# A fused Mamba block and 16-expert layer on one core: the late expert weights in small waited pieces, and a last group normalised on VectorE

## What is computed

```
attn:  xz = layernorm(x) @ in_proj.T;  x_in, z = split(xz)
       u = silu(causal_conv4(x_in) + conv_b);  delta, B, C = u @ x_proj.T
       h_t = h_{t-1} * exp(-delta_t) + B_t u_t;  y_t = h_t . C_t
       out = (y * silu(z)) @ out_proj.T + x
ffn:   the two best of 16 experts for each token, weights w from their softmax
       for each expert e:  y = (silu(x @ W1[e]) * (x @ W3[e])) @ W2[e]
                           out += w_e * (layernorm(y) * gamma[e] + beta[e])
```

## Time and profile before

| | us |
|---|---|
| median of 3 runs (971.96 to 977.71) | 974.45 |
| the profiled execution, its own time | 974.93 |
| its span, first to last instruction | 973.1 |
| TensorE busy | 940.0 (97%) |
| VectorE busy | 722.8 (74%) |
| ScalarE busy | 689.5 (71%) |
| GpSimd busy | 620.4 (64%) |

### The profile page before, as it was taken

How to read it: one execution, slowest core, us unless ns; L and a number is a source line. 1 busy time by engine, 2 the same in 40 slices (tenths; PEclk the granted TensorE clock), 3 DMA queues, 4 the chain that set the end, 5 groups by cost and what they waited for, 6 DMA issues and landing times.

```text
span 973.1 us, 26657 instructions
## 1 busy us (share of the span) xinstructions
PE 940.0 (97%) x7207; PEld 833.9 (86%) x7207; DVE 722.8 (74%) x2524; ACT 689.5 (71%) x1358; POOL 620.4 (64%) x813
## 2 busy tenths in 40 slices
PE   8999999999999999998879999999999999999994
PEld 5777887788887887887879999999999999999951
DVE  2379999999999998898623767776767677677656
ACT  3777787777778778765115777777777778778536
POOL 2445777777778777775541666666666666566647
PEclk9999999999999999999988999999999999999997
DMA  4001323121111111110865211111111111111075
GB/s 136 12 12 34 93 93 97 58 62 48 55 56 53 53 43 42 42 42 22 324 238 175 87 44 51 49 51 46 49 50 48 47 50 49 42 53 50 18 293 225
DMA packets 54159, 75.25 MB, mean 77 GB/s; under 512 B 11103, under 2 KB 32865, under 8 KB 53376
## 3 DMA queue, kind: packets, MB, share of 16 engines
q1 hardware_dynamic: 42784, 54.87, 18.4%
q0 software_dynamic: 8672, 16.93, 4.8%
q10 hardware_dynamic: 2560, 1.75, 0.6%
HBM read 47.09 MB, written 27.41 MB: 77 GB/s over the span
## 4 chain that ended last, share of the span: by engine, by line
PE 79%; DVE 7%; POOL 6%; issue 5%; DMA 1%; ACT 1%; POOLq 0%; DVEq 0%; SPq 0%; ACTq 0%
PE pA L1886 11%; PE pR L1886 11%; PE pA L1472 11%; PE pB L1894 6%; PE pY L1894 5%; PE pY L1586 4%; PE pB L1498 3%; PE pB L1632 3%; PE pA L1487 3%; PE pY L1622 3%; PE pA L1443 3%; POOL chosen_scratch L656 2%; PE pY L1605 2%; PE pY L1554 2%; PE pR L1570 2%
## 5 line engine op out<-in xcount | busy, mean ns | idle before, releaser
L656 POOL DMA_INDIRECT chosen_scratch<-yo,got_id x143 | 146.8, 1027 | 93.7 <-issue 87.9
L961 ACT ACTIVATE stage<-w_sb 128x1024 f32 x143 | 151.2, 1057 | 55.7 <-issue 55.6
L1358 DVE TENSOR_TENSOR hidT<-pR,sil 128x512 f32<-128x512 f32 x143 | 98.9, 692 | 81.0 <-ACT sil L956 60.8
L595 POOL DMA_INDIRECT slots_scratch<-xrow,send_at x128 | 134.7, 1052 | 35.3 <-issue 31.3
L1886 PE MATMUL pA<-xsT,stage 128*128 128x128 f32 x1144 | 151.3, 275 | 0.4 <-ACT xsT L945 0.4
L1886 PE MATMUL pR<-xsT,stage 128*128 128x128 f32 x1144 | 151.1, 275 | 0.0
L1886 PEld LDWEIGHTS pA<-xsT,stage 128*128 128x128 f32 x1144 | 139.2, 192 | 0.7 <-ACT xsT L945 0.6
L1886 PEld LDWEIGHTS pR<-xsT,stage 128*128 128x128 f32 x1144 | 139.0, 192 | 0.0
L1472 PE MATMUL pA<-xn,taps 128*128 128x512 f32 x256 | 129.8, 594 | 1.0 <-ACT xn L722 1.0
L646 POOL TENSOR_TENSOR ers<-eve,neg_half 128x1 f32<-128x1 f32 x143 | 81.7, 571 | 57.2 <-DVE eve L1370 40.0
L956 ACT ACTIVATE sil<-pA 128x512 f32<-128x512 f32 x143 | 85.3, 596 | 26.5 <-PE pA L1886 21.7
(11 more groups left out here) (198 smaller groups left out, 2102.0 us busy)
## 6 DMA issues: line engine op xcount, KB each, us to landing
got<-slots_scratch SPq DMA_DIRECT2D x143, 65.0 KB, 1.9
w_sb<-chosen_scratch SPq DMA_DIRECT2D x16, 512.0 KB, 5.4
w_sb<-in_w_dram SPq DMA_DIRECT2D x1, 6144.0 KB
xin<-in_x_dram SPq DMA_DIRECT2D x16, 256.0 KB
xr<-in_x_dram SPq DMA_DIRECT2D x16, 256.0 KB, 3.1
x_scratch<-x SPq DMA_DIRECT2D x16, 256.0 KB
w_sb<-in_w_dram SPq DMA_DIRECT2D x4, 1024.0 KB, 7.2
fx<-x_scratch SPq DMA_DIRECT2D x1, 4096.0 KB
```

What stands on the lines that cost most here:

```text
L595: eng.indirect_dma_start(slots_d, bass.IndirectOffsetOnAxis(ap=send_at[:, s % 2, k, t:t + 1], axis=0), xrow[:, s % 2, k, t, :], None).then ...
L656: eng.indirect_dma_start(chosen_d, bass.IndirectOffsetOnAxis(ap=got_id[:, j % NGOT:j % NGOT + 1], axis=0), yo[:, q, :], None, bounds_check ...
L961: eng.activation(stage[:, j % NSTAGE, :, :].rearrange("p k f -> p (k f)"), w13_sb[:, bass.ds(e, 1), :, :].rearrange("p o k f -> p (o k f)" ...
L1358: eng.tensor_tensor(hidT[:, p, :], pR[:, p, :], sil[:, p, :], ALU.mult).then_inc(hid_ready, 1)
```

## The change

- `load_late` is replaced. `load_middle(e0, e1)` issues the weights of two experts (1 MB) and first waits until the piece before has landed (`w13_loaded`). The first, (4, 6), waits also for the state products of the last sequence (`ys_mm`). Five such pieces take experts 4 to 13; then come `store_x1(15)`, expert 14 alone, and `load_last`: expert 15, gamma, and beta, the last one after a wait until gamma has landed.
- `tail_at` is computed in the last call of `positions`, right behind the counts and ahead of `placed` and `pos`, no longer behind `count_i`.
- `fnm` is gone. GpSimd multiplies the mean itself with `frs`, and the second operation subtracts the product from `shift3` where it added before.
- Group 15 is normalised by VectorE with four `tensor_scalar`s from PSUM, added by VectorE, and stored by a DMA of ScalarE's queue; GpSimd's addition, ScalarE's four activations and SyncE's store of it are gone.
- 42 fillers in place of 46.

```diff
-DVE_ADDS = tuple(range(1, 15, 2))
+DVE_ADDS = tuple(range(1, 16, 2))
...
+            def load_middle(e0, e1):
+
+                if e0 == 4:
+                    eng.wait_ge(ys_mm, 2 * NS)
+                eng.wait_ge(w13_loaded, 16 * (e0 // 2 - 1))
+                load_w13(e0, e1)
+
+            def load_last():
+                eng.wait_ge(y_step, 11 * NS)
+                eng.wait_ge(w13_loaded, 16 * 7)
+                load_w13(15, NE)
+                for k, v in enumerate((gamma, beta)):
+                    if k:
+                        eng.wait_ge(gb_loaded, 16 * k)
                     eng.dma_start(gb[:, k, :, :], ...).then_inc(gb_loaded, 16)
...
             store_x1(14)
-            load_late()
+            load_middle(4, 6)
+            load_middle(6, 8)
+            load_middle(8, 10)
+            load_middle(10, 12)
+            load_middle(12, 14)
             store_x1(15)
+            load_middle(14, 15)
+            load_last()
...
-                eng.tensor_tensor(fshift[:, h % 2, c], fnm[:, h % 2, c], frs[:, h % 2, c], ALU.mult).then_inc(f_rstd, 1)
+                eng.tensor_tensor(fshift[:, h % 2, c], fmv[:, h % 2, c, 0:1].rearrange("p t o -> p (t o)"), frs[:, h % 2, c], ALU.mult).then_inc(f_rstd, 1)
...
-                eng.tensor_tensor(fshift[:, h % 2, c], fshift[:, h % 2, c], shift3[:, g:g + n, :].rearrange("p g t -> p (g t)"), ALU.add).then_inc(f_rstd, 1)
+                eng.tensor_tensor(fshift[:, h % 2, c], shift3[:, g:g + n, :].rearrange("p g t -> p (g t)"), fshift[:, h % 2, c], ALU.subtract).then_inc(f_rstd, 1)
...
-            eng.wait_ge(w13_loaded, 32)
+            eng.wait_ge(w13_loaded, 16 * 8)
...
-            for h in range(len(PARTS)):
+            for h in range(len(PARTS) - 1):
                 last_norm(h)
+            eng.wait_ge(f_o_dve, len(DVE_ADDS) + 1)
+            eng.dma_start(ov[NG - 1, :, :, :], fx1[:, NG - 1, :, :]).then_inc(f_stored, 16)
...
+                if s == NS - 1:
+                    eng.wait_ge(rank_read, NS)
+                    eng.tensor_scalar(tail_at[:, :], running[:, :], slot_no[:, 0:1], None, ALU.add).then_inc(tail_ready, 1)
...
-                eng.tensor_scalar(fnm[:, h % 2, c], fmv[:, h % 2, c, 0:1].rearrange("p t o -> p (t o)"), -1.0, None, ALU.mult).then_inc(f_var, 1)
...
+            h = len(PARTS) - 1
+            g = NG - 1
+            eng.wait_ge(f_rstd, 3 * h + 3)
+            eng.wait_ge(f_o_dve, len(DVE_ADDS))
+            for t in range(NT4):
+                eng.tensor_scalar(fn[:, h % 2, 0, t, :], sum_bank(g)[:, tile(t)], frs[:, h % 2, t:t + 1], fshift[:, h % 2, t:t + 1], ALU.mult, ALU.add).then_inc(f_last, 1)
+            eng.wait_ge(f_last, NT4)
+            eng.tensor_tensor(fx1[:, g, :, :], fn[:, h % 2, 0, :, :], fx1[:, g, :, :], ALU.add).then_inc(f_o_dve, 1)
...
-            keep_warm(46)
+            keep_warm(42)
```

More of the change, by code:

```diff
@@ L256, in sandwich @@
         fve = sb("fve", [P, 2, 2 * NT4])
-        fnm = sb("fnm", [P, 2, 2 * NT4])
         frs = sb("frs", [P, 2, 2 * NT4])
@@ L316, in sandwich @@
         cv = chosen_d.rearrange("(k g p t) d -> g p k (t d)", p=P, t=NT4, k=2)
+        ov = out.rearrange("s (p t) d -> s p t d", t=NT4)
         sum_bank = lambda g: w13_sb[:, 0, 0, :] if g == 0 else (pA, pB, pR, pY)[g % 8 // 2][:, g % 2, :]
@@ L349, in sandwich @@
         f_sum, f_moments, f_var, f_rstd, f_n, f_o = sem("f_sum"), sem("f_moments"), sem("f_var"), sem("f_rstd"), sem("f_n"), sem("f_o")
-        f_o_dve = sem("f_o_dve")
+        f_o_dve, f_last = sem("f_o_dve"), sem("f_last")
         f_stored = sem("f_stored")
@@ L380, in load_late @@
                 for k, v in enumerate((gamma, beta)):
+                    eng.dma_start(gb[:, k, :, :], v.rearrange("(o e) d -> o e d", o=1).broadcast_to([P, NE, D])).then_inc(gb_loaded, 16)
+            def load_middle(e0, e1):
[10 more added lines that the diff above has]
+                        eng.wait_ge(gb_loaded, 16 * k)
                     eng.dma_start(gb[:, k, :, :], v.rearrange("(o e) d -> o e d", o=1).broadcast_to([P, NE, D])).then_inc(gb_loaded, 16)
@@ L483, in _ @@
                 eng.wait_ge(stored[q], len(range(q, NSLOT, 4)) * 16)
-            ov = out.rearrange("s (p t) d -> s p t d", t=NT4)
             eng.wait_ge(staged, NSLOT)
@@ L491, in _ @@
                 eng.dma_start(w13_sb[:, g, :, :], cv[g, :, :, :]).then_inc(f_loaded[g % 4], 16)
-            for g in range(NG):
+            for g in range(NG - 1):
                 if g in DVE_ADDS:
@@ L669, in last_rstd @@
                 g, n = PARTS[h]
-                eng.wait_ge(f_var, 2 * h + 2)
+                eng.wait_ge(f_var, h + 1)
                 if h >= 2:
@@ L691, in _ @@
                     last_add(h - 1)
-            last_add(len(PARTS) - 1)
         @block.scalar
@@ L979, in last_norm @@
                     if h >= 3:
-                        eng.wait_ge(f_o_dve, min(h - 1, len(DVE_ADDS) + 1))
+                        eng.wait_ge(f_o_dve, h - 1)
                 for q in range(PARTS[h][1]):
@@ L1328, in _ @@
             r.link(eng.tensor_tensor(count_i[:, :], running[:, :], region_sb[:, :], ALU.subtract))
-            eng.tensor_scalar(tail_at[:, :], running[:, :], slot_no[:, 0:1], None, ALU.add).then_inc(tail_ready, 1)
             r.link(eng.memset(ones_e[:, :], 1.0))
@@ L1409, in last_aggr @@
                 eng.wait_ge(f_moments, 8 * g + 4 * n)
-                wait_past(eng, f_var, 2 * (h - 1))
+                wait_past(eng, f_rstd, 3 * (h - 1) - 1)
                 eng.sem_inc(dve_passed, 1)
@@ L1418, in last_var @@
                 eng.wait_ge(f_moments, 8 * (g + n))
-                wait_past(eng, f_rstd, 3 * (h - 1))
                 eng.tensor_scalar(fve[:, h % 2, c], fmv[:, h % 2, c, 1:2].rearrange("p t o -> p (t o)"), EPS, None, ALU.add).then_inc(f_var, 1)
-                eng.tensor_scalar(fnm[:, h % 2, c], fmv[:, h % 2, c, 0:1].rearrange("p t o -> p (t o)"), -1.0, None, ALU.mult).then_inc(f_var, 1)
             def last_add(h):
```

## The result

| | us |
|---|---|
| changed kernel, median of 7 runs (979.3 to 983.48) | 981.79 |
| kernel before, 7 runs on the same chip (971.96 to 977.71) | 975.72 |
| ratio, 95% interval | 1.0068 (1.0046 to 1.0090) |
| profiled execution of the changed kernel, its span | 982.6, 980.8 |

The change makes the kernel about 6 us slower, 0.7%. The forecast was 977.2. The time lies inside the range of 970.5 to 985.5, but in the upper third of it, and it is slower by more than 0.5%, a case to which I had given 0.33. Of the 4.6 us between forecast and median, 1.3 are the kernel before itself: its seven runs here have a median of 975.72, the three that I had counted from have 974.45.

The account below looks back on a forecast made before the run. TensorE was taken to bound the kernel, with SyncE's path 4 us behind it between the stages. +1.7 + 2.5 - 0.5 - 0.9 = +2.8 on the profiled 974.9, median 0.5 lower: 977.2 us, range 970.5 to 985.5.

Parts of the forecast that it names:

- SyncE's sum: Between stages 1 and 2: SyncE's waited loads, then blank rows, delay the first tile's transposition to 523.0, plus 1.7 us.
- Rival 3: Dear pieces in SyncE's load queue: 6.1 us per 1 MB, tile 8.3 us late, +9.4 in all, 984; chance 0.26.
- expert 15 with gamma: Last waited load in SyncE's queue, 1.5 MB: 2.3 + 3.9 + 0.4 = 6.6 us, gamma landed at 508.9.
- rival 2: Cheap pieces in SyncE's load queue: a landing's fixed part is 1.9 us, about -3 in all, 971.5; chance 0.27.
- What SyncE covers: End of stage 1: GpSimd, ScalarE's blank rows and table ready some 3 us earlier, costed at nothing since SyncE is last.
- hidden: Rival between the stages: SyncE through early, fillers and sends decide, stage 2 starts near 511; -11.7 us, 963; chance 0.07.
- GpSimd's stall: End of stage 1: smaller packets end the 2.21 us stall at the second send; power up to 1.9 us earlier.
- rival 4: Stage 1 unmoved, the stall not from large packets: changes nothing while SyncE is last; inside the forecast, no chance given.
- The clock between the stages: Start of stage 2: TensorE, idle 12 us before the tile, works 5 us at half speed; plus 2.5 us (1.7 to 3.5).
- Stage 3: Last stage: minus 0.5 us without fnm, minus 0.9 with group 15 on VectorE, its four PSUM operations of 1.12 us running freely.
- the bound that I had named: End of stage 3, group 15 moved to VectorE: -1.3 us, the fast bound around the forecast of minus 0.9.
- The rhythm: Stage 3 from frs to frs: without fnm 0.08 us less per part, seven times, minus 0.5 us.

Follow-up runs that it names:

- e10: Changed kernel with experts 4 to 13 loaded in ten waited pieces of 512 KB instead of five of 1 MB; 994.30 us, ratio 1.0193 to the kernel before.
- e5: The changed kernel run again, unaltered, on another chip; 983.17 us, ratio 1.0089 to the kernel before.
- e1: Kernel before with only the change's loads and their waits; 982.98 us, ratio 1.0123 to the kernel before.
- e6: Changed kernel with 84 fillers for 50 between the table and the first tile; 982.14 us, ratio 1.0085 to the kernel before.
- e3: Changed kernel with all its load pieces but no waits for landings between them; 973.29 us, ratio 1.0027 to the kernel before.
- e4: Changed kernel without the last three waits for landings (before expert 14, expert 15 and beta); 975.75 us, ratio 1.0053 to the kernel before.
- e2: Changed kernel with the old loads (load_late) put back, all other edits kept; 972.17 us, ratio 1.0004 to the kernel before.
- e7: Changed kernel with the old loads and 54 fillers for 48 ahead of stage 3's first pair sum; 976.54 us, ratio 1.0016 to the kernel before.
- e9: Changed kernel with experts 4 to 13 in three waited pieces (2, 2 and 1 MB) instead of five; 978.51 us, ratio 1.0033 to the kernel before.
- e12: Kernel before with the change's stage 3 edits, 56 fillers for 48 before the first pair sum, 42 for 50 before the first tile; 970.88 us, ratio 1.0005.
- e11: Kernel before with the change's stage 3 edits and 56 fillers for 48 ahead of the first pair sum; 974.94 us, ratio 0.9993 to the kernel before.
- e8: Kernel before with 30 fillers for 50 ahead of the first tile; 974.75 us, ratio 1.0005 to the kernel before.

## Why the prediction was right and wrong

**SyncE's sum.** The mechanism was right, and the price of a piece too: 5.23 us for 5.1, from 471.8 on for 472.5. (Rival 3 put a piece at 6.1, so it did not happen, though the time came out on its side.) Expert 14 took 4.4 for 4.3. The term that was mis-sized is expert 15 with gamma, 6.6 by my sum and 8.6 in the trace, 2.0 us; I had made it of one fixed part and 3.9 us of bytes. GpSimd's sends (501.5 to 510.4) fell into it: I had them land at 508, on the strength of the stall that should vanish. That they are the reason fits e10, where the same two transfers go out at 517.6, behind the sends, and take 7.0 us, and e5, e1 and e6, where they lie among the sends and take 8.8, 9.1 and 10.5. From beta to the first blank row it is 1.9 where I took 0.9; the eight stores then take 7.5 for 8.8. The rest is as worked out: 524.95 for 523.0. The rule of the Trainium skill ("DMA: Bandwidth & Descriptors", "Anatomy of one DMA — SWDGE (gpsimd) path"), a fixed 2.0 us beside the bytes at 436 GB/s on GpSimd's path, gives estimates of 3.2, 4.4 and 6.8 us for 512 KB, 1 MB and 2 MB; SyncE's waited pieces took 3.9, 5.2 and 8.4, so here the measurement stands against it, and rival 2 fell with it.

**What SyncE covers.** That SyncE's queue would now decide when the first tile comes was right. Before, SyncE had time to spare, for it stood waiting for the addresses of the blank rows:

```profile
SPq L320 <- DVE tail_at L1329: 12.7, 1, 12.7
```

The waits could use up these 12.7 us for nothing, and what they take beyond delays the tile. The same wait is 9.6 us in e3 and 2.5 in e4; in the change the addresses are there at 499.7, and SyncE comes for them 11.6 us later. I said that without SyncE the path would go by fillers and sends, and called its fall to 511 the rival "hidden"; e3, with nothing waited for and on a chip without the pauses, transposes at 513.71, as its fillers end.

**GpSimd's stall.** This step was wrong. The 2.21 us ahead of the second send are in all fourteen traces, 2.21 to 2.27 each, also in e3, which moved 422 to 425 GB/s at that time, and in the change, whose packets I had called smaller. It belongs to that place in the program; what it is stays open. With it fell everything that was to be 1.9 us earlier, and rival 4, which I had put inside the forecast, is what happened.

In the change's trace the power is 1.0 us late and the ranking and the last sends some 1.9. This is not the edits: e3 and e10 have the same edits in this part, but their clock fell where it fell before (see the last section), and in them the power starts at 483.26 and 483.46 (before: 483.56) and the last sequence's sends at 499.42 and 499.75 (before: 499.59). TensorE's gap ahead of the transposition is 2.28 and 2.35 us there, the old 1.46 and the 0.9 of the four fillers; in the change it is 3.90, where I had it shrink to 0.6. I had costed this part at nothing because SyncE covers it, and covered it was, except for the sends that fell among the last loads.

**The clock between the stages.** +2.85 for +2.5: right in size, though I had stage 2 without slack, and e6 shows that some 0.8 of it would be lost again at the ninth tile if the clock stayed up. The working had a wrong part: I let the fillers end at 511 and TensorE idle for 12 us. They end at 522.7, because pauses and a low clock stretch them as they did before, and 2.25 us of idle time were enough.

**Stage 3.** The four operations are not held beside GpSimd's addition, as the rule of the Trainium skill that I had set beside them says ("VectorE: DVE Perf Modes", "Why PSUM operands drop a tier"), but they take 1.37 us for my 1.12. From the start of the last `frs` to the end of the last addition it is 3.77 us, before 4.52: minus 0.75 for the 0.9 of my sum. The end as a whole gave -1.3, the bound that I had named, by something that stands in no term of the sum. Before, the chain that ended last closes with GpSimd's queue at the end of the program (line 105):

```profile
968.80 1.30 POOLq L105
```

This instruction (a DRAIN) starts with GpSimd's last addition and lasts 4.09 us, to 972.89, while the last store has landed at 972.10. In the change it lasts as long, but starts with the addition of group 14 and is over at 980.29, ahead of the last store's landing at 980.36. So moving group 15 off GpSimd took some 0.6 us of waiting for GpSimd's queue out of the end. That gain was luck.

The rhythm gave +0.35 for -0.5. Most parts are faster, 3.59 to 3.64 us from `frs` to `frs` for 3.68. But at one part VectorE's addition and GpSimd's power now start at the same moment, and the power takes 2.19 us in place of 1.64. The ten further traces with these edits of stage 3 (e2 to e7, e9 to e12) have one such power of 2.18 or 2.19, and 26.02 to 26.05 us for the whole stretch. Every other power of this size takes 1.64 or 1.65 us in all fourteen traces, and where an addition of VectorE runs beside it, this starts 0.17 to 0.25 us later. That the common start is the cause is read from this; no run moves the addition alone.

```profile
959.57 2.19 POOL L694 TENSOR_TENSOR frs<-fve,neg_half 128x8 f32<-128x8 f32 x1 [0.35 <-DVE fve L1442]
...
963.72 1.64 POOL L694 TENSOR_TENSOR frs<-fve,neg_half 128x8 f32<-128x8 f32 x1
```
```profile
959.32 0.17 DVE L1442 TENSOR_SCALAR fve<-fmv 128x8 f32<-128x8 f32 x1
959.57 0.69 DVE L1447 TENSOR_TENSOR fx<-fn,fx 128x512 f32<-128x512 f32 x1
```

The intervals from `frs` to `frs` that end and begin with that power are 3.85 and 4.15 us, 0.65 more than two of the old ones, and the other five gain 0.3. I had looked at one interval and multiplied by seven; a rhythm that shifts two engines against each other has to be laid out part by part.

**Not in the sum.** 2.1 us: the clock at the first pair sum, and 0.25 ahead of the load. Against the profiled execution I forecast +2.8 and it was +7.7; the difference of 4.9 is 2.0 from the first tile, 0.35 from its clock, 2.1 here, and 0.45 from stage 3. All four are on the slow side, and it is the width of the range, drawn for dearer pieces, that still holds the time.

## What to carry over

A wait for a landing costs a fixed part, about 2.4 us here, whatever is moved, and everything that stands behind it in that queue pays it: count the waits between now and the next thing that anyone needs, take off the time that the queue has to spare (12.7 us here), and pace transfers only in a queue that has nothing else to do. Lay out the queue behind the waits step by step, since eight small stores and their landing were late with it, and ask what the late loads will meet there. Where an idle time of TensorE grows to some 2 us, add the low clock that follows it (1.3 to 2.85 us at the start of stage 2). Fillers that end with the arrival avoid it; fillers that end behind it delay the start by as much as they are late. When an engine's last work goes away, look also at what waits for that engine at the end.

## What the runs showed of the hardware

**Pauses that depend on the chip.** In nine traces (before, the change, e5 to e11) the engines' instructions stop several times between about 505 and 514 us, while GpSimd sends and ScalarE's queue writes blank rows, in some of them SyncE's too. In the five others (e1 to e4, e12) they do not. TensorE over the same five us before and in e12 (columns as in the earlier trace rows):

```profile
506.00:511.00 5.00, 1.34 (x5) 1.13 (x5) 0.00 (x0) 0.00 (x0) 2.81 (x3) 0.81 0.36 107
```
```profile
506.00:511.00 5.00, 5.00 (x47) 5.00 (x46) 0.00 (x0) 0.00 (x0) 2.44 (x3) 1.00 0.67 122
```

The copy of the table on VectorE waited 9.23 us before, and SyncE's eight blank rows took 13.06, 8.29 in e12; my reading of that row, that other traffic slowed it, does not hold, for in e12 ScalarE's stores and GpSimd's sends go out beside it as well:

```profile
511.04 0.68 DVE L1349 CAST slot_table<-pA 1x512 int32<-1x512 f32 x1 [9.23 <-remote]
```
```profile
499.48 8.29 SPq L321 DMA_DIRECT2D slots_scratch<-blank  x8
```

The nine traces are from chips on which the kernel before takes 975.5 to 975.9 us, the five from chips on which it takes 970.7 to 970.9. This fits the loads' cost, 12.1 us on one of the second kind and 6 to 8 for the whole change on the first: behind SyncE's waits the pauses cost little, while the kernel before has its fillers last there. No trace of the unchanged kernel was taken on a chip of the second kind, so that its 5 us less there are the pauses is argued from e12, which differs from e11 by eight fillers and transposes its first tile at 515.23 in place of 521.90. What stops the instructions is open.

**A low clock that moves.** In stage 1 TensorE falls to 1.2 GHz for some 3.4 us at places that differ from trace to trace, in kernels that are the same up to there: in the first 30 us, at 450 to 452, or at 475 to 477. Where only the last of these occurs (before, e3, e10, e12) the 2 MB load is issued at 461.1 to 461.5; with one of the others at 462.4 to 462.7 (the change, e4, e5, e7, e11), with both at 464.1 to 464.6 (e1, e2, e6, e8, e9). So 0.8 us of the difference between the two profiled executions at that load, 462.35 for 461.52, are this and not the change.
